# Cross-attention of a decoder block: turned maximum, softmax reciprocals and projection loads moved

## The chip, the cores and the metric

The kernel runs on one core of a Trainium2 chip. The metric is the device time of one execution in microseconds, the median over runs; lower is better.

## The reference

A decoder block with norms behind its residual sums: self-attention with fake quantisation to 8 bits, cross-attention, and a feed-forward net with low-rank additions. Eight batches of 512 tokens with 512 channels. The change is in the cross-attention, here cut to its core:

```python
q = (query @ Wq + bq).reshape(B, Nq, H, D).transpose(0, 2, 1, 3)      # B 8, Nq 512, H 16, D 32
k = (key_value @ Wk + bk).reshape(B, Nkv, H, D).transpose(0, 2, 1, 3)
v = (key_value @ Wv + bv).reshape(B, Nkv, H, D).transpose(0, 2, 1, 3)
attn = jnp.clip(jnp.einsum('bhqd,bhkd->bhqk', q, k) * scale, -CLAMP, CLAMP)
attn = jax.nn.softmax(attn, axis=-1)
x = jnp.einsum('bhqk,bhkd->bqhd', attn, v).reshape(B, Nq, Cq)
return x @ Wo + bo          # then: x2 = layernorm(x1 + this)
```

## The kernel before

The block is cut into stages with a barrier of all five engines between them; intermediate tensors go through device memory. Order within a stage is the order of each engine's own instruction list, tied by semaphores. SP issues nearly all the DMAs, in the order of its list, so a wait on SP holds every DMA behind it.

**Attention (between barriers 9 and 10).** 128 heads are 32 groups (GROUPS) of four. A group's queries and keys come as stacks of float16 halves (Qs, Ks; four slots), its values as vX (two slots). For each key tile c of four (NT), TensorE does in this order (group, line 981 on): score pair u = 0 of a head that is LEAD = 5 heads ahead, in banks 0 and 1, for the maximum alone (score_pair, L926); a quarter of the sums or values of the group before (values_of, L973); transposed key scores of this group (key_scores, L934) for two heads; score pair u = 1; key scores of the two other heads; minus the maximum added to all four by a matmul with ones (take_max, L942); another quarter of values_of. In the first two tiles values_of makes the softmax sums (bank 7), in the last two the values (bank 6). Behind the fourth tile the next group's maxima, which DVE has split in three bfloat16 parts (split_max, six small steps, L1593 to L1598, behind the third tile's reductions), are turned by four transposes (turn_max, L953) into bank 7, and ACT copies them to nmT (L1229).

DVE reduces each score pair to maxima (max_pair, L1583), which frees banks 0 and 1 for the next pair, and clips the exponentials of a tile in one step for all four heads (clip, L1604). ACT does the exponentials (L1235), the copies of values (values_out, L1223, at the start of a group) and sums (sums_out, L1216). SP's turn for a group (group_dma) waits for the last scores of that group, issues eight stack loads (L577) for the group four later, the next V load (L585), a store of the sums (L597) and a store of the undivided values (L591). After the last group all sums are loaded at once (L621), inverted by DVE (L1636) and stored (L625).

**Projection (between barriers 10 and 11).** SP loads Wo and bo (L632, L633), and per batch the values oK (L640), four broadcasts of reciprocals recK (L643) and the residual x1 into xK (L645). GpSimd multiplies oK by recK (L732), TensorE multiplies by Wo (L1024), DVE adds bo (L1646), adds the product (L1650) and norms; SP stores x2 (L649). Two slots each; a load of a batch waits for the store of x2 two batches before. ACT issues the loads of the two feed-forward weights, 4 MB each, behind the first xK loads (L1250).

Of the kernel before, what the change touches and what calls it, by code (L numbers as in the profile page):

```python
# [15 lines left out]
P = 128  # L16
# [14 lines left out]
XD = 32  # L31
# [42 lines left out]
def decoder(nc, x, ctx_768, g_ln, b_ln, w_qkv, w_out, log_temp, Wq, bq, Wk, bk, Wv, bv, Wo, bo,  # L74
# [22 lines left out]
    with ExitStack() as ctx:  # L97
# [234 lines left out]
        cX = Carve()  # L332
        Qs = cX(F16, 4, G, T)
# [5 lines left out]
        all_sums = cX(F32, T)  # L339
# [5 lines left out]
        nmT = cX(BF16, T)  # L345
# [3 lines left out]

        cK = Carve()  # L350
        Wo_s = cK(F32, KC, D)
        bo_s = cK(F32, D)
        oK = cK(F32, 2, KC, T)
        xK = cK(F32, 2, NT, D)
# [30 lines left out]
        recK = Carve(cW.at)(F32, 2, KC, T)  # L385
# [5 lines left out]
        def _(sp):  # L391
# [195 lines left out]
            def store_group(i, par):  # L587
                sp.wait_ge(S("oX_evac"), i + 1)
# [3 lines left out]

            def store_sums(i, par):
                sp.wait_ge(S("sumS_done"), i + 1)
                hold(sp)
                dst = sums_scr[i] if isinstance(i, int) else sums_scr[bass.ds(i, 1)].rearrange("a g t -> (a g) t")
                sp.dma_start(dst, sumS[0:P:XD, par, :]).then_inc(S(f"sums_stored{par}"), 16)  # L597
# [15 lines left out]
            with sp.Fori(1, GROUPS // 4 - 1) as j:  # L613
                for r in range(4):
                    group_dma(j * 4 + r, r)
            for i in range(GROUPS - 4, GROUPS):
                group_dma(i, i % 4)
            store_sums(GROUPS - 1, 1)
            for par in (0, 1):
                sp.wait_ge(S(f"sums_stored{par}"), 8 * GROUPS)  # L620
            sp.dma_start(all_sums, sums_scr.rearrange("a g t -> (a g) t")).then_inc(S("all_sums_in"), 16)  # L621
            for i in (GROUPS - 2, GROUPS - 1):
                store_group(i, i % 2)
            sp.wait_ge(S("rec_done"), 1)
            sp.dma_start(rec_scr.rearrange("a g t -> (a g) t"), all_sums).then_inc(S("rec_stored"), 16)  # L625
            for par in (0, 1):
                sp.wait_ge(S(f"oX_stored{par}"), 8 * GROUPS)
            sp.wait_ge(S("rec_stored"), 16)
            barrier(sp, 10)


            sp.dma_start(Wo_s, chunk(Wo)).then_inc(S("wI_in"), 16)  # L632
            sp.dma_start(bo_s, bo.rearrange("(a n) -> a n", a=1).broadcast_to([P, D])).then_inc(S("wI_in"), 16)  # L633

# [1186 lines left out]
```

## Time and profile before

| | us |
|---|---|
| median of 3 runs | 3690.12 (3690.01 to 3691.11) |
| profiled execution, time | 3690.49 |
| profiled execution, span | 3688.7 |
| TensorE matmul busy in the span | 2745.9 (74%) |
| DVE busy | 2574.5 (70%) |
| ACT busy | 1463.6 (40%) |
| GpSimd busy | 146.4 (4%) |
| attention, first to last matmul | 2153.2 to 2798.4 |
| projection, first to last matmul | 2834.2 to 3001.0 |

The profile is one execution; its rows are in microseconds from the start of the span. A timeline row gives start, length, engine, line, what is written from what, how many were merged, and in brackets how long the engine was idle before and what ended that. The mean granted clock of TensorE is a share of 2.4 GHz; 0.50 is 1.2 GHz. Busy shares are averages over stages with different limits, so each stage is read by itself.

### The profile page before, as it was taken

What the parts mean: (1) busy time and instruction counts of PE and PEld (TensorE: products, weight loads), DVE (VectorE), ACT (ScalarE), POOL (GpSimd) and SP (SyncE); (2) the same over time, 40 slices, a digit from 0 to 9 for tenths busy, and PEclk for the clock granted to TensorE, in tenths of its full rate; (3) what the DMA queues carried; (4) which work ended last, traced back from release to release, by engine and by line L of the source; (5) the groups of instructions that cost most, each with busy time, mean ns of one, the idle gap of its engine ahead of it and who ended that gap; (6) DMA issues with size and microseconds to landing.
All of it is one profiled execution on the core that took longest, in us unless ns stands there. A gap on an engine that the chain in (4) does not pass through costs nothing. (4 is left out here: it accounts for less than half of the span.)

```text
span 3688.7 us, 46276 instructions
## 1 busy us (share of the span) xinstructions
PE 2745.9 (74%) x13160; PEld 1067.8 (29%) x13160; DVE 2574.5 (70%) x4657; ACT 1463.6 (40%) x2397; POOL 146.4 (4%) x148
## 2 busy tenths in 40 slices
PE   1189999566664666664599969999995645999998
PEld 1134322111111433331244412222222223444443
DVE  6877799989887988884355547777773576455444
ACT  0000444489887988871122224444441001212221
POOL 0000333000000000000000000000001210000000
PEclk8599999555555989887799969999997877999999
DMA  5221221223232443434544433323325531001000
GB/s 199 74 91 46 92 116 78 103 102 112 100 105 90 135 126 125 129 111 183 193 165 166 175 86 84 84 75 82 86 63 194 182 121 35 24 23 36 33 23 23
DMA packets 199676, 375.20 MB, mean 102 GB/s; under 512 B 23680, under 2 KB 109696, under 8 KB 187136
## 3 DMA queue, kind: packets, MB, share of 16 engines
q1 hardware_dynamic: 195344, 357.03, 29.5%
q10 hardware_dynamic: 4208, 16.78, 1.2%
q8 instruction: 46, 0.75, 0.1%
q14 instruction: 78, 0.64, 0.1%
HBM read 218.02 MB, written 155.71 MB: 101 GB/s over the span
## 5 line engine op out<-in xcount | busy, mean ns | idle before, releaser
L1289 DVE TENSOR_REDUCE stats<-bank 128x1024 f32 (+1 forms) x352 | 407.9, 1216 | 65.5 <-PE bank L765 32.0
L1154 ACT ACTIVATE arena<-arena,scale 128x512 bf16<-128x512 int8 x512 | 410.1, 802 | 103.1 <-DVE arena L1476 94.4
L825 PE MATMUL bank<-arena 64*128 64x512 bf16 x512 | 306.2, 605 | 173.9 <-DVE arena L1471 138.8
L1583 DVE TENSOR_REDUCE arena<-bank 128x2 f32<-128x1024 f32 x256 | 312.8, 1222 | 136.3 <-PE bank L926 136.3
L1471 DVE CUSTOM_DVE_ANT_0 arena<-bank,arena,fac 128x512 int8<-128x512 f32 x512 | 353.9, 747 | 38.3 <-issue 17.8
L1169 ACT ACTIVATE arena<-arena,scale 128x512 f32<-128x512 int8 x512 | 366.4, 801 | 27.9 <-DVE arena L1497 14.8
L1235 ACT ACTIVATE arena<-bank 128x1024 f32<-128x1024 f32 x256 | 248.2, 1021 | 322.5 <-PE bank L942 322.5
L973 PE MATMUL bank<-arena 128*32 128x512 f32 x2048 | 272.0, 607 | 40.8 <-issue 32.7
L765 PE MATMUL bank<-arena 128*128 128x512 bf16 x1024 | 246.7, 386 | 59.9 <-DVE arena L1419 52.4
L845 PE MATMUL bank<-identb,arena 128*128 128x128 bf16 x2048 | 155.9, 237 | 172.1 <-DVE arena L1506 171.7
L1267 ACT ACTIVATE arena<-bank,arena,fac 128x512 f32<-128x512 f32 x128 | 99.5, 777 | 456.2 <-PE bank L1097 456.2
L1506 DVE TENSOR_SCALAR arena<-arena 128x512 bf16<-128x512 f32 x512 | 226.3, 481 | 43.5 <-ACT arena L1169 40.1
L1105 PE MATMUL bank<-arena 128*128 128x512 f16 x1024 | 242.0, 379 | 1.2 <-DVE arena L1767 0.8
L1094 PE MATMUL bank<-arena 128*128 128x512 f16 x1024 | 241.9, 379 | 0.0
L1766 DVE TENSOR_SCALAR arena<-arena 128x512 f16<-128x512 f32 x128 | 54.7, 427 | 260.0 <-ACT arena L1267 260.0
L845 PEld LDWEIGHTS bank<-identb,arena 128*128 128x128 bf16 x2048 | 132.2, 107 | 236.0 <-DVE arena L1506 146.3
L926 PE MATMUL bank<-arena 128*128 128x512 f16 x512 | 161.8, 399 | 42.3 <-DVE arena L1583 28.8
L1024 PE MATMUL bank<-arena 128*128 128x512 f32 x256 | 119.2, 628 | 83.4 <-POOL arena L732 83.4
L825 PEld LDWEIGHTS bank<-arena 64*128 64x128 bf16 x512 | 51.8, 101 | 428.3 <-DVE arena L1471 417.3
L1142 ACT ACTIVATE arena<-bank,floor_c,fac 128x1024 int8<-128x1024 f32 x96 | 115.6, 1205 | 150.1 <-PE bank L765 95.6
L1604 DVE TENSOR_SCALAR arena<-arena 128x2048 f32<-128x2048 f32 x128 | 155.8, 1217 | 13.3 <-ACT arena L1235 13.3
L934 PE MATMUL bank<-arena 128*128 128x512 f16 x512 | 157.2, 391 | 0.3
(189 smaller groups left out, 3585.1 us busy)
## 6 DMA issues: line engine op xcount, KB each, us to landing
dq_scr<-arena SPq DMA_DIRECT2D x128, 256.0 KB, 2.0
arena<-dq_scr SPq DMA_DIRECT2D x128, 256.0 KB, 2.7
arena<-half_scr SPq DMA_DIRECT2D x256, 128.0 KB, 2.8
qkv_scr<-arena SPq DMA_DIRECT2D x8, 3072.0 KB, 9.7
arena<-in_x SPq DMA_DIRECT2D x16, 1024.0 KB, 7.0
arena<-qkv_scr SPq DMA_DIRECT2D x128, 128.0 KB, 2.2
o_scr<-arena SPq DMA_DIRECT2D x64, 256.0 KB, 2.9
arena<-o_scr SPq DMA_DIRECT2D x8, 2048.0 KB, 9.2
```

The lines of the kernel that those rows point to most:

```text
L765: last = mm(dst, wqkv_q[:, k, P * u:P * u + P], hq[:, k, :], start=k == 0, stop=k == KC - 1)
L825: return mm(dst, qE[r, h // 2, P * t:P * t + P], kE[r, h // 2, :], start=True, stop=True)
L845: last = nc.tensor.transpose(PT[s % 2][:, j, P * t:P * t + P], aG[:, s % 2, t, P * j:P * j + P], identb[:, :])
L973: last = mm(bank[XD * g:XD * g + XD, 7 if k < 2 else 6, :], w, eT[:, par, g, c, :], start=c == 0, stop=c == NT - 1)
L1094: mm(dst, Wf[:, k, P * s:P * s + P], xx[:, par, k, :], start=k == 0 and n == 0, stop=False)
L1105: mm(bank[:, t, :], gg[:, f % 3, P * t:P * t + P], Wp[:, f, :], start=f == 0 and n == 0, stop=False)
L1154: last = A(e_dump[:, NT * (h % 2) + t, :], dq8[:, h % 4, t, :], ACT.Exp, bias=negm_b[:, par, c:c + 1], scale=scale[:, S_DOTS:S_DOTS + 1], ...
L1169: A(eG[:, s % 2, t, :], dqG[:, s % 4, t, :], ACT.Exp, bias=negm_g[:, par, c:c + 1], scale=scale[:, S_DOTS:S_DOTS + 1]).then_inc(S("eG_done ...
L1235: A(eT[:, r % 2, 2 * a:2 * a + 2, c, :], bank[:, 2 + 2 * a:4 + 2 * a, :], ACT.Exp, scale=XSCALE / HALF ** 2).then_inc(S("eX_done"), 1)
L1289: return V.tensor_reduce(dst, src, ax, ALU.max, apply_absolute_value=True)
L1471: V.tensor_tensor_reduce(dq8[:, s, t, :], bank[:, 4 * (h % 2) + t, :], floor_row, fac[:, C_DOTS:C_DOTS + 1], -3.0e38, ALU.add, ALU.max, ac ...
L1583: V.tensor_reduce(mxX[:, mp, hs, 2 * u:2 * u + 2], bank[:, 0:2, :], AX.X, ALU.max).then_inc(S("sX_red"), 1)
```

## The change

In the attention: the turn of the next maximum moves on TensorE from behind the last key tile to inside it, ahead of its key scores, and its copy on ACT ahead of that tile's exponentials, with nmT in two slots. The split on DVE is cut in two parts of three steps, with a reduction between. Clips of the first and last tile are done in halves. The sums of a group go through memory one group at a time: store, load spread over 128 partitions with 16 columns each, reciprocal on DVE in the group two later, store, broadcast back to recB, and GpSimd multiplies the evacuated values before they are stored. The last two groups are inverted and multiplied by DVE. In the projection nothing is divided any more; its tiles lie at the top of the arena, and its weights and first two batches are loaded before the last four groups. Values of batch b+2 are loaded once batch b's matmuls are done, x1 once its x2 is stored.

```diff
             def store_group(i, par):
-                sp.wait_ge(S("oX_evac"), i + 1)
+                sp.wait_ge(S("oX_ready"), i + 1)
                 hold(sp)
...
+            def load_spread(i, par):
+                sp.wait_ge(S(f"sums_stored{par}"), i * 8 + 16 - 8 * par)
+                hold(sp)
+                sp.dma_start(sums16, spread(sums_scr, i)).then_inc(S("sums16_in"), 16)
+
+            def store_rec(i):
+                sp.wait_ge(S("rec_done"), i + 1)
+                hold(sp)
+                sp.dma_start(spread(rec_scr, i), sums16).then_inc(S("rec_stored"), 16)
+
+            def load_rec(i, par):
+                sp.wait_ge(S("rec_stored"), i * 16 + 16)
+                hold(sp)
+                for g in range(G):
+                    row = rec_scr[i, g:g + 1, :] if isinstance(i, int) else rec_scr[bass.ds(i, 1), g, :]
+                    sp.dma_start(recB[XD * g:XD * g + XD, par, :], row.broadcast_to([XD, T])).then_inc(S(f"rec_in{par}"), 16)
...
             def group_dma(i, r):
-                if not (isinstance(i, int) and i + 4 >= GROUPS):
+                known = isinstance(i, int)
+                if not (known and i + 4 >= GROUPS):
                     load_stacks(i + 4, r)
-                if not (isinstance(i, int) and i + 1 >= GROUPS):
+                if not (known and i + 1 >= GROUPS):
                     load_v(i + 1, (r + 1) % 2)
-                if not (isinstance(i, int) and i < 1):
+                if not (known and i < 2):
+                    store_rec(i - 2)
+                if not (known and i < 3):
+                    store_group(i - 3, (r + 1) % 2)
+                if not (known and i < 1) and not (known and i == GROUPS - 1):
                     store_sums(i - 1, (r + 1) % 2)
-                if not (isinstance(i, int) and i < 2):
-                    store_group(i - 2, r % 2)
+                if not (known and i < 2):
+                    load_rec(i - 2, r % 2)
+                if not (known and i < 1) and not (known and i == GROUPS - 1):
+                    load_spread(i - 1, (r + 1) % 2)
...
+            sp.dma_start(Wo_s, chunk(Wo)).then_inc(S("wI_in"), 16)
+            sp.dma_start(bo_s, bo.rearrange("(a n) -> a n", a=1).broadcast_to([P, D])).then_inc(S("wI_in"), 16)
+            for b in (0, 1):
+                load_values(b, b)
+                load_x1(b, b)
             for i in range(GROUPS - 4, GROUPS):
                 group_dma(i, i % 4)
...
+            def after_batch(b, par):
+                sp.wait_ge(S("wo_mm"), b * NT + NT)
+                hold(sp)
+                load_values(b + 2, par)
+                store_x2(b, par)
+                sp.wait_ge(S(f"x2_stored{par}"), b * 8 + 32 - 8 * par)
+                load_x1(b + 2, par)
...
+            def divide(i, par):
+                pool.wait_ge(S(f"rec_in{par}"), (i * 8 + 16 - 8 * par) * G)
+                pool.wait_ge(S("oX_evac"), i + 1)
+                hold(pool)
+                nc.gpsimd.tensor_tensor(oX[:, par, :], oX[:, par, :], recB[:, par, :], ALU.mult).then_inc(S("oX_ready"), 1)
...
                     if previous:
                         values_of(i - 1, (r + 1) % 2, c, 0)
+                    if c == NT - 1 and not (isinstance(i, int) and i == GROUPS - 1):
+                        turn_max(i + 1)
                     key_scores(i, r, c, 0)
...
                     if previous:
                         values_of(i - 1, (r + 1) % 2, c, 1)
-                if not (isinstance(i, int) and i == GROUPS - 1):
-                    turn_max(i + 1)
...
             def group(i, r):
-                if not (isinstance(i, int) and i < 2):
-                    values_out(i - 2, r)
-                act.wait_ge(S("nmT_mm"), i + 1)
-                A(nmT, turned_max, ACT.Copy).then_inc(S("nmT_ready"), 1)
                 for c in range(NT):
+                    if c == 0 and not (isinstance(i, int) and i < 2):
+                        values_out(i - 2, r)
...
+                    if c == NT - 1 and not (isinstance(i, int) and i == GROUPS - 1):
+                        max_turned(i + 1, 1 - r)
...
+            def invert(i):
+                dve.wait_ge(S("sums16_in"), i * 16 + 16)
+                V.reciprocal(sums16, sums16).then_inc(S("rec_done"), 1)
...
-                        if u == 0:
-                            clip_before(i, r, c)
-                    if c == 2 and not (isinstance(i, int) and i == GROUPS - 1):
-                        split_max(i + 1, (r + 1) % 2)
+                        if c == 0 and not first:
+                            clip(i - 1, 1 - r, NT - 1, u)
+                        if c == 1:
+                            clip(i, r, 0, u)
+                        if (c, u) == (2, 0):
+                            clip(i, r, 1, None)
+                        if (c, u) == (2, 1) and not last:
+                            split_max(i + 1, 1 - r, True, False)
+                        if (c, u) == (3, 0) and not last:
+                            split_max(i + 1, 1 - r, False, True)
+                        if (c, u) == (3, 1):
+                            clip(i, r, 2, None)
+                        if (c, u) == (0, 1) and not (isinstance(i, int) and i < 2):
+                            invert(i - 2)
...
-            clip(GROUPS - 1, 1, NT - 1)
-            dve.wait_ge(S("all_sums_in"), 16)
-            V.reciprocal(all_sums, all_sums).then_inc(S("rec_done"), 1)
+            for a in (0, 1):
+                clip(GROUPS - 1, 1, NT - 1, a)
+            for i in (GROUPS - 2, GROUPS - 1):
+                dve.wait_ge(S("sumS_done"), i + 1)
+                link(V.reciprocal(sumS[:, i % 2, :], sumS[:, i % 2, :]))
+                dve.wait_ge(S("oX_evac"), i + 1)
+                dve.wait_ge(S("oX_ready"), i)
+                V.tensor_tensor(oX[:, i % 2, :], oX[:, i % 2, :], sumS[:, i % 2, :], ALU.mult).then_inc(S("oX_ready"), 1)
```

## Rows read from the trace of the kernel before

**Rows 1.** Windows: one group; length, busy by engine (instructions), granted clock, DMA share, GB/s.
```profile
2507.24:2526.50 19.26, 17.50 (x120) 4.22 (x116) 15.12 (x18) 9.23 (x12) 0.00 (x0) 1.00 0.29 82
```

**Rows 2.** Timeline around the start of a group, TensorE, ACT and SP.
```profile
2505.92 0.40 PE L942 MATMUL bank<-arena 3*128 3x512 bf16 x4
2506.62 3.66 SPq L577 DMA_DIRECT2D arena<-half_scr  x8
2507.25 0.40 PE L953 MATMUL bank<-identb,arena 128*128 128x128 bf16 x4
2509.37 1.06 PE L973 MATMUL bank<-arena 128*32 128x512 f32 x8 [1.30 <-issue]
2511.16 0.57 SPq L597 DMA_DIRECT2D sums_scr<-arena  x1
```

**Rows 3.** Timeline of a middle key tile, score pairs and reduction.
```profile
2513.09 0.61 PE L926 MATMUL bank<-arena 128*128 128x512 f16 x2
2515.07 0.59 PE L926 MATMUL bank<-arena 128*128 128x512 f16 x2
2517.35 0.60 PE L926 MATMUL bank<-arena 128*128 128x512 f16 x2
2517.99 1.23 DVE L1583 TENSOR_REDUCE arena<-bank 128x2 f32<-128x1024 f32 x1 [0.77 <-PE bank L926]
```

**Rows 4.** Timeline of a last key tile.
```profile
2502.39 0.60 PE L926 MATMUL bank<-arena 128*128 128x512 f16 x2
2502.44 0.17 DVE L1593 TENSOR_SCALAR arena<-arena 128x16 f32<-128x16 f32 x1 [0.18 <-DVE arena L1583]
```

**Rows 5.** Waits of SP over 2200 to 2780: total us, times, longest.
```profile
SPq L231 <- PE bank L942: 359.1, 27, 16.8
```

**Rows 6.** DMAs: stacks' landing times; two issues at the seam (KB, landing); one broadcast set.
```profile
DMA to landing us min/median/max: 2.1/2.8/4.3
...
arena<-sums_scr SPq DMA_DIRECT2D x1, 256.0 KB, 2.9
rec_scr<-arena SPq DMA_DIRECT2D x1, 256.0 KB, 2.0
...
2807.46 2.60 SPq L643 DMA_DIRECT2D arena<-rec_scr  x4
```

**Rows 7.** Windows of one us behind group 30, columns as in rows 1.
```profile
2776.00:2777.00 1.00, 0.00 (x0) 0.00 (x0) 0.89 (x1) 1.00 (x3) 0.00 (x0) 1.00 0.72 158
2777.00:2778.00 1.00, 0.84 (x5) 0.23 (x8) 0.34 (x1) 0.06 (x1) 0.00 (x0) 0.53 0.82 311
...
2780.00:2781.00 1.00, 1.00 (x7) 0.11 (x5) 0.00 (x0) 0.00 (x0) 0.00 (x0) 0.77 0.00 0
```

**Rows 8.** Timeline of the seam between attention and projection.
```profile
2790.47 7.95 PE L973 MATMUL bank<-arena 128*32 128x512 f32 x72
2792.54 1.23 DVE L1604 TENSOR_SCALAR arena<-arena 128x2048 f32<-128x2048 f32 x1 [1.93 <-ACT arena L1235]
2800.43 3.35 DVE L1636 RECIPROCAL arena<-arena 128x512 f32<-128x512 f32 x1 [6.66 <-DMA arena<-sums_scr]
2834.23 6.23 PE L1024 MATMUL bank<-arena 128*128 128x512 f32 x9 [35.82 <-POOL arena L732]
```

**Rows 9.** Projection: its window, columns as in rows 1, and timeline rows.
```profile
2834.20:3001.10 166.90, 119.25 (x256) 51.24 (x256) 91.73 (x228) 0.00 (x0) 36.59 (x28) 0.84 0.63 206
...
2903.31 0.37 SPq L649 DMA_DIRECT2D x_scr<-arena  x1
2921.50 4.96 DVE L1646 TENSOR_TENSOR arena<-arena 128x512 f32<-128x512 f32 x4 [4.40 <-DMA arena<-x_scr]
2950.02 2.49 DVE L1646 TENSOR_TENSOR arena<-arena 128x512 f32<-128x512 f32 x4
2979.41 20.76 PE L1024 MATMUL bank<-arena 128*128 128x512 f32 x48
```

More of the change, by code:

```diff
@@ L338, in decoder @@
         sumS = cX(F32, 2, T)
-        all_sums = cX(F32, T)
+        recB = cX(F32, 2, T)
+        sums16 = cX(F32, G * T // P)
         mxX = cX(F32, 2, G, NT)
@@ L649, in store_x2 @@
                 sp.dma_start(at4(x2_scr, b), xK[:, par]).then_inc(S(f"x2_stored{par}"), 16)
-            ahead(sp, load_values, store_x2)
+            def after_batch(b, par):
[5 more added lines that the diff above has]
+                load_x1(b + 2, par)
+            with sp.Fori(0, NB // 2 - 1) as j:
+                after_batch(j * 2, 0)
+                after_batch(j * 2 + 1, 1)
+            store_x2(NB - 2, 0)
+            store_x2(NB - 1, 1)
             for par in (0, 1):
@@ L941, in take_max @@
                     q = slice(XD * g, XD * g + 3)
-                    last = mm(bank[:, 2 + g, :], ones_b[q, :], nmT[q, :], start=False, stop=True)
+                    last = mm(bank[:, 2 + g, :], ones_b[q, :], nmT[q, r % 2, :], start=False, stop=True)
                     if g % 2:
@@ L1601, in clip @@
[L1601 to L1611 removed]
+                if first:
+                    dve.wait_ge(S("sX_red"), i * 8 + 8)
+                    if not (isinstance(i, int) and i == 0):
+                        dve.wait_ge(S("nmT_mm"), i)
+                    hold(dve)
+                    ch.link(V.tensor_scalar(capX, mxX[:, mp], XSCALE / HALF ** 2, CLIP_SPAN - CLAMP, ALU.mult, ALU.max))
+                    ch.link(V.tensor_scalar(negX, capX, CLAMP, -(HALF ** 2) / XSCALE, ALU.min, ALU.mult))
+                    ch.link(V.tensor_copy(slots[:, :, :, 0], by_tile(negX)))
@@ new lines, in split_max, with clip @@
+                ch.n = 3
+                if second:
+                    ch.link(V.tensor_tensor(by_tile(restX), by_tile(negX), slots[:, :, :, 0], ALU.subtract))
+                    ch.link(V.tensor_copy(slots[:, :, :, 1], by_tile(restX)))
+                    V.tensor_tensor(slots[:, :, :, 2], by_tile(restX), slots[:, :, :, 1], ALU.subtract).then_inc(S("nm_ready"), 1)
+                    ch.end()
+            def clip(i, r, c, a):
+                heads = slice(0, G) if a is None else slice(2 * a, 2 * a + 2)
+                n = 2 if a is None else 1
+                dve.wait_ge(S("eX_done"), i * 8 + 2 * c + (a or 0) + n)
+                e = eT[:, r, heads, c, :]
+                V.tensor_scalar(e, e, CLIP_FLOOR, 1.0, ALU.max, ALU.min).then_inc(S("clipped"), n)
@@ L1613, in group @@
+            def invert(i):
+                dve.wait_ge(S("sums16_in"), i * 16 + 16)
+                V.reciprocal(sums16, sums16).then_inc(S("rec_done"), 1)
             def group(i, r):
+                first, last = (isinstance(i, int) and i == k for k in (0, GROUPS - 1))
                 for c in range(NT):
```

108 lines of the change are left out of this document (38 added, 70 removed).

## The prediction

> **What bounds the kernel now.** I read the page's slices first, then the windows by stage, the timeline of one attention group, the waits of the DMA queue, and the timeline of the seam behind the attention. In the cross-attention a group of four heads takes 19.26 us with TensorE busy 17.50, DVE 15.12, ACT 9.23 [rows 1]. Within a group a middle key tile takes 4.26 us, from 2513.09 to 2517.35, and the next maximum reduction starts 0.64 us behind its score pair, which it had waited for [rows 3]: TensorE is the bound there. Four tiles and the turn (0.23 us) would be 17.27; the group has two holes besides. At its start TensorE waits for the evacuation of the turned maximum: turn at 2507.25, next value matmul 2509.37; the first tile takes 5.6 us in place of 4.26 [rows 2]. In the last tile six small DVE steps stand ahead of the reduction that frees the score banks, and it takes 4.86 us (2502.39 to 2507.25) [rows 2, 4]. Together 2.0 us. Behind the attention TensorE stands still from 2798.42 to 2834.23, 35.8 us, and the projection then takes until 3001.1 with TensorE busy 119 of 167 us at a mean clock of 0.84 [rows 8, 9].
>
> **The turn and the splits.** The turn moves into the last tile, ahead of its key scores, so its evacuation is hidden: minus 1.35 us. But it needs the second half of the split, which now stands behind the reduction of that tile's first score pair. Counted from the third tile's first matmul: the last tile's begins at 4.26, its reduction runs about 4.98 to 6.20, three small steps of 0.17 to 0.23 us with gaps take 0.70; the first of them is in [rows 4], so the turn can begin at 7.0. TensorE is there at 5.80: pair, value matmuls and two key scores take 1.98 (2513.09 to 2515.07), the key scores alone some 0.44 of it [rows 3]. It waits 1.2 us, where it lost 0.6. Net minus 0.8 a group: 18.5 us if nothing else waits. The clip in halves and the split in parts only fill DVE's idle 0.6 to 0.8 us behind each reduction; with TensorE as the bound they give nothing more.
>
> **The way of the sums through memory.** This is the term that decides. SP runs its list in order. Its turn for a group begins when the group's last scores are done (first stack issue at 2506.62, 0.70 behind the start of the last maximum matmuls), and before the change it then has slack: over 27 groups it waited 359 us for that event, 13.3 each [rows 2, 5]. Call this start s; the next group's first score pair, F, is at s + 0.63 once the turn is gone from there (0.33 for the maxima and 1.0 for the values behind 2505.92). In the changed list the load of group i-2's sums for the reciprocal stands last in the turn of group i-1, and DVE waits for it in group i behind its second reduction. So it is not a whole group of slack but the first few us of a group. The chain:
> - eight stack issues and the V load: 4.54 us until the next issue (2506.62 to 2511.16) [rows 2], now the store of the previous reciprocals;
> - SP waits for that store to land. No row shows it beside the stacks: alone a store to this tensor took 2.0, a stack under the same burst 2.8 in the median, 4.3 at most [rows 6]. I take 2.8, as this one is queued behind the burst. The stores of values and sums are issued in that time;
> - four row broadcasts: 2.60 for four such issues; eight stack issues took 3.66, so 1.83 is the low end [rows 2, 6]; 3.2 the high end, by estimate from these;
> - the load itself: 2.9 for the load of all sums [rows 6], 2.0 to 4.3 as bounds; small gaps between issues 0.3.
>
> Sum 4.54 + 2.8 + 2.6 + 2.9 + 0.3 = 13.1 us behind s (10.7 to 16.6). DVE gets there on its own at F + 4.5 = s + 5.1: two reductions, each 0.64 behind its pair, the second pair at F + 1.98, and half a clip of 0.61. So DVE waits some 8 us (5.6 to 11.5) every group. Queued behind it is the next reduction, and behind that, on TensorE, the second score pair of the second tile. The reciprocal of 16 columns is 3.35 / 32 [rows 8] plus a fixed part, 0.3 us; then 1.22 for the reduction and 0.12. The pair starts at s + 14.8 = F + 14.2; from there 2.28 us finish the tile (2515.07 to 2517.35) and 4.26 + 5.70 the other two. Group: 26.4 us, 7.1 more than now.
>
> ACT has a wait of the same kind: evacuating the values of group i-2 needs group i-4's store, which has moved one turn later and behind the stacks: about s + 5.4 + 2.8, evacuation and first exponentials at s + 9.9. TensorE needs these for the key scores of the second tile, which it reaches before the late score pair at s + 14.8: hidden. The GpSimd division takes 1.3 us (36.59 / 28) [rows 9], in a time when its core has nothing else, and nobody waits for it but SP one turn later.
>
> **The clock.** For 7.6 us TensorE would have two matmuls. In this trace an idle stretch of 1.7 us behind group 30 was enough: granted 1.00 in the idle us, 0.53 in the next, 0.77 in the fourth [rows 7], so 3.7 us at 1.2 GHz. That loses 1.9 us of TensorE's work, and TensorE is the bound behind the wait. Group: 28.3 us.
>
> The sum: groups 3 to 28 have the full chain, 26 x (28.3 - 19.26) = 235. Group 2 has no reciprocals to store ahead, 2.7 us shorter: +6. Groups 29 and 30 have no stacks ahead, 3.9 us shorter: +10. Group 31 +1, groups 0 and 1 together -1.6. Attention +251.
>
> **Seam and projection.** Operands, bias and the first two batches are loaded in the attention. After its last matmul comes on DVE the tail of two reciprocals of 3.35 and two products of 0.7; the first starts behind the last clip (2792.54 and 1.23), 4.6 us before the end, so the last product ends 3.8 behind it, and with a store of 2.9 and the barrier it is 7.3 us [rows 6, 8]. The projection itself: 48 matmuls in 20.76 us [rows 9] are 0.43 each, 32 a batch, 13.8 us; eight batches 110.1, plus 1.9 for a slow clock at the start and 3 for x1 tiles that arrive late beside the two 4 MB weight loads, which now start at once (an estimate, 0 to 8). DVE is busy 91.7 us in eight batches, 11.5 each, under 13.8. From a store of x2 to the adds on the x1 that waits for it is 18.2 us now (2903.31 to 2921.50), with 2 MB of values and reciprocals ahead in the queue; without them it should fit in the other batch's 13.8. From the last attention matmul to the last projection matmul: 7.3 + 115 = 122.3, now 202.7. Gain 80. The removed GpSimd scaling stood between load and matmul and is in this figure. Cover for the early loads: 5.25 MB at about 0.3 MB a us is 17 us, in front of group 28's turn, inside a group's length; without that cover they cost some 4 us once.
>
> Profiled execution: span 3688.7, time 3690.5, against a median of 3690.1. 3690.5 + 251 - 80 = 3861 us. The unknown transfers alone move it from 3791 to 3955.
>
> The Trainium skill, DMA: Bandwidth & Descriptors, section "Anatomy of one DMA", gives a DMA a fixed cost of about 2.0 us that does not grow with size, most of it the receipt of the write. By that both waits would be 2.0, the group about 1.7 us shorter, and the time about 3815; the lone store agrees at 2.0, the stacks in the burst do not (2.8).
>
> **Rivals.**
> - A: the wait is there but the clock holds. For it: granted clock 1.00 all through a group that has a hole of 1.3 us [rows 1, 2]. Against it: rows 7, with a shorter idle time than I expect. Group 26.4 us, attention +195, time 3805; with the shortest transfers 3737.
> - B, on the other side: the transfers are covered, DVE finds its sums in place, and the change does what it says. Then 18.5 us a group, attention -25, time 3585. It decides at a chain of s + 8.8 us: there the group is 22.1 us and pays back the 80. For it: 13 us of slack on SP. Against: this slack lies ahead of s, not behind it, and the stacks alone take 3.7.
> - C: GpSimd's division holds DVE up as well. Beside such products DVE's four bias adds took 4.96 us, alone 2.49 [rows 9]. Up to 1.3 us a group, 26 x 1.3 = 34: 3895. Against: it falls where DVE waits or reads PSUM. The Trainium skill, SBUF — State Buffer, section "Who interferes with whom", has the two engines share a port pair that one instruction holds whole; the trace agrees, with 4.96 against 2.49.
>
> **Chances.** Forecast 0.60 (3790 to 3955), A 0.22 (3737 to 3830), C 0.08, B 0.10. The range of 8 in 10 takes the forecast's and A's cases but for their far ends: 3750 to 3930. About 0.2% is what a measurement of this kernel tells from no change. Slower by over that 0.90 (forecast, A, C), within it 0.01, faster 0.09 (B, with a little left for something between).
>
> **What would show it.** A DVE wait of some 8 us for a load of the sums in each of groups 2 to 28, and TensorE idle behind it; group length near 28 us; granted clock down to about 0.5 for 3 to 4 us in each group. The turn waiting about 1.2 us for DVE in the last tile. ACT's evacuation of the values waiting for a store of two groups before, with nobody behind. At the seam under 10 us, and the projection at 13.8 us a batch without TensorE's holes of 15 us. Wrong it would be if SP reaches the load of the sums within 6 us, if two landings together take under 2 us, or if DVE's wait lies where TensorE has work that needs neither score banks nor exponentials.

## The result and the profile of the changed kernel

The changed kernel takes 3807.3 us in the median (3804.1 to 3810.4), the kernel before 3690.6 beside it: a ratio of 1.031, interval 1.030 to 1.032. It is slower by 117 us, inside the range of the prediction and 54 us under its 3861. The profiled execution took 3804.1 us with a span of 3802.1, which is 113.4 more than before. All of it lies in two places: the attention, first to last matmul, takes 844.4 us instead of 645.2 (plus 199.2), and from its last matmul to the last of the projection it is 116.9 instead of 202.7 (minus 85.8).

Windows of the changed kernel: 25 groups of the attention (turn to turn), one group of them, three stretches within it, and the projection. Columns as in rows 1.
```profile
2260.52:2932.24 671.72, 506.79 (x2900) 111.57 (x2901) 388.50 (x525) 235.21 (x275) 31.52 (x25) 0.85 0.28 76
2611.22:2636.82 25.60, 19.56 (x116) 4.41 (x117) 15.50 (x21) 9.33 (x11) 1.26 (x1) 0.87 0.27 73
2622.00:2623.00 1.00, 0.18 (x1) 0.13 (x2) 0.00 (x0) 1.00 (x2) 0.00 (x0) 0.77 0.37 127
2623.00:2629.00 6.00, 3.94 (x14) 0.74 (x16) 3.76 (x5) 1.29 (x2) 1.26 (x1) 0.50 0.07 17
2629.00:2630.00 1.00, 1.00 (x9) 0.11 (x2) 0.00 (x0) 1.00 (x2) 0.00 (x0) 0.82 0.00 0
3001.90:3113.50 111.60, 111.53 (x256) 49.21 (x256) 86.54 (x231) 0.00 (x0) 0.00 (x0) 0.99 0.68 254
```
A group takes 671.72 / 25 = 26.9 us where it took 19.26 [rows 1]. TensorE is busy 506.79 / 25 = 20.3 us of it, before 17.5, at a mean clock of 0.85, before 1.00. So of the 7.6 us more, 2.8 are the same matmuls run slower and 4.8 are idle time (6.6 now, 1.8 before). The projection is now full: 111.53 busy of 111.60, where it was 119 of 167 [rows 9].

Waits of the changed kernel over the same 25 groups: who waits for whom, us in total, times, longest.
```profile
DVE arena L1650 <- DMA arena<-sums_scr: 159.7, 25, 7.6
ACT arena L1254 <- DMA oT_scr<-arena: 159.3, 25, 8.1
PE bank L968 <- ACT arena L1270: 78.2, 25, 4.8
PE bank L960 <- DVE arena L1620: 59.7, 25, 2.9
PE bank L987 <- DVE arena L1638: 27.2, 25, 1.2
SPq L231 <- PE bank L976: 408.7, 25, 16.8
```
Every group has the new wait of DVE's reciprocal (L1650) for the load of its sums, 6.4 us in the mean. It has a second one that looks just as large: ACT's evacuation of the values (L1254) for a store of two groups before. SP itself still stands idle 408.7 us for the last scores of a group, 16.3 each, as in [rows 5]: its slack is there, but behind the list and not ahead of it.

Timeline of one group of the changed kernel, the rows in the order of the chain. L987 is the turn, L960 a score pair, L968 the key scores, L1620 the maximum reduction, L1650 the reciprocal; on SP L578 is the stacks, L586 V, L613 the store of reciprocals, L592 and L603 those of values and sums, L620 the broadcasts, L608 the load of sums.
```profile
2611.22 0.38 PE L987 MATMUL bank<-identb,arena 128*128 128x128 bf16 x4 [1.01 <-DVE arena L1638]
2613.52 3.65 SPq L578 DMA_DIRECT2D arena<-half_scr  x8
2614.15 0.61 PE L960 MATMUL bank<-arena 128*128 128x512 f16 x2
2617.44 0.35 SPq L586 DMA_DIRECT2D arena<-v_scr  x1
2618.17 0.38 SPq L613 DMA_DIRECT2D rec_scr<-arena  x1
2618.91 0.35 SPq L592 DMA_DIRECT2D oT_scr<-arena  x1
2620.72 1.91 SPq L620 DMA_DIRECT2D arena<-rec_scr  x4
2621.25 0.60 ACT L1254 ACTIVATE arena<-bank 128x512 f32<-128x512 f32 x1 [6.05 <-DMA oT_scr<-arena]
2622.82 1.04 PE L968 MATMUL bank<-arena 128*128 128x512 f16 x2 [2.80 <-ACT arena L1270]
2622.88 0.36 SPq L608 DMA_DIRECT2D arena<-sums_scr  x1
2624.50 1.26 POOL L764 TENSOR_TENSOR arena<-arena 128x512 f32<-128x512 f32 x1 [25.39 <-DMA arena<-rec_scr]
2624.52 0.25 DVE L1650 RECIPROCAL arena<-arena 128x16 f32<-128x16 f32 x1 [5.93 <-DMA arena<-sums_scr]
2624.69 1.17 DVE L1620 TENSOR_REDUCE arena<-bank 128x2 f32<-128x1024 f32 x1
2625.92 1.04 PE L960 MATMUL bank<-arena 128*128 128x512 f16 x2 [2.06 <-DVE arena L1620]
2628.28 1.57 PE L1004 MATMUL bank<-arena 128*32 128x512 f32 x8
2636.82 0.38 PE L987 MATMUL bank<-identb,arena 128*128 128x128 bf16 x4 [1.18 <-DVE arena L1638]
```
SP's turn starts at s = 2613.52, the next scores at F = 2614.15, 0.63 later. The reciprocal's sums are there at 2624.52 = s + 11.0. Behind it come the reduction and, at 2625.92, the late score pair, F + 11.8. TensorE had two holes ahead of it, 2.80 and 2.06 us, with one key score pair between them. The eight value matmuls at L1004 behind take 1.57 us at the lower clock and 1.06 to 1.07 elsewhere in the group. The turn waits 1.0 to 1.2 us for DVE's last split step (L1638).

Timeline of the seam in the changed kernel.
```profile
2988.69 7.93 PE L1004 MATMUL bank<-arena 128*32 128x512 f32 x72
2998.75 0.69 DVE L1691 TENSOR_TENSOR arena<-arena 128x512 f32<-128x512 f32 x1
3001.96 111.53 PE L1055 MATMUL bank<-arena 128*128 128x512 f32 x256 [5.33 <-POOLq L235]
```
The hole of 35.8 us [rows 8] is 5.3, and the 256 matmuls of the projection run in one piece.

### The profile page after: what moved, and what is told of

Its sections match the earlier page's. It is cut to its first block and busy times, and to the rows that moved or that the text cites. A ratio compares the mean times of both kernels' runs of the same rounds, so it can differ in the third digit from the quotient of the medians.

```text
span 3802.1 us, 46990 instructions
## 1 busy us (share of the span) xinstructions
PE 2799.9 (74%) x13113; PEld 1070.7 (28%) x13160; DVE 2583.6 (68%) x4754; ACT 1468.5 (39%) x2397; POOL 143.2 (4%) x146
## 3 DMA queue, kind: packets, MB, share of 16 engines
q1 hardware_dynamic: 204832, 356.46, 28.3%
## 5 line engine op out<-in xcount | busy, mean ns | idle before, releaser
L1620 DVE TENSOR_REDUCE arena<-bank 128x2 f32<-128x1024 f32 x256 | 311.7, 1218 | 151.3 <-PE bank L960 144.1
L1004 PE MATMUL bank<-arena 128*32 128x512 f32 x2048 | 297.7, 661 | 0.0
L960 PE MATMUL bank<-arena 128*128 128x512 f16 x512 | 181.5, 442 | 100.4 <-DVE arena L1620 86.7
L1125 PE MATMUL bank<-arena 128*128 128x512 f16 x1024 | 243.1, 381 | 0.0
L1136 PE MATMUL bank<-arena 128*128 128x512 f16 x1024 | 242.0, 379 | 1.2 <-DVE arena L1822 0.7
L968 PE MATMUL bank<-arena 128*128 128x512 f16 x512 | 174.1, 427 | 80.1 <-ACT arena L1270 79.8
L1646 DVE TENSOR_SCALAR arena<-arena 128x1024 f32<-128x1024 f32 (+1 forms) x192 | 166.7, 869 | 4.5 <-ACT arena L1270 4.5
L1549 DVE TENSOR_SCALAR arena<-bank 128x2048 bf16<-128x2048 bf16 x128 | 155.8, 1217 | 1.9 <-PE bank L879 0.7
```

Source lines behind the costliest of these rows:

```text
L1004: last = mm(bank[XD * g:XD * g + XD, 7 if k < 2 else 6, :], w, eT[:, par, g, c, :], start=c == 0, stop=c == NT - 1)
L1125: mm(dst, Wf[:, k, P * s:P * s + P], xx[:, par, k, :], start=k == 0 and n == 0, stop=False)
L1136: mm(bank[:, t, :], gg[:, f % 3, P * t:P * t + P], Wp[:, f, :], start=f == 0 and n == 0, stop=False)
L1620: V.tensor_reduce(mxX[:, mp, hs, 2 * u:2 * u + 2], bank[:, 0:2, :], AX.X, ALU.max).then_inc(S("sX_red"), 1)
```

## The experiments

My theory: the whole loss is the two waits through memory that SP's list puts into the first microseconds of a group, DVE's first of all, with the clock behind it. The rivals: the wait is there but something else holds the group (ACT's wait, GpSimd's division, the split of the DVE work); or the clock has no part in it. The kernel before was measured beside every experiment, with medians of 3691.1 to 3692.5.

**The reciprocal later on DVE.** The kernel change with one condition moved: the reciprocal comes in the last key tile in place of the first.
```diff
-                        if (c, u) == (0, 1) and not (isinstance(i, int) and i < 2):
+                        if (c, u) == (3, 0) and not (isinstance(i, int) and i < 2):
                             invert(i - 2)
```


> Edit: the reciprocal of group i-2's sums moves on DVE from behind the second reduction of group i to behind the seventh (last tile); SP's list stays. DVE's wait for the sums (6.4 us a group in the changed kernel's trace) should be gone, ACT's wait for the store of the values of group i-4 stays. Theory (two waits side by side, the longer hides the shorter): key scores of the second tile are then late by 2.9 us; group 21.4 us while the clock holds, 3664 us; 23.2 us with a dip of the clock, 3711 us. Rival (DVE's wait alone makes the loss, ACT's is free): 18.5 us a group, 3584 us. Rival (DVE's place in the list doesn't matter, the memory traffic does): 3807 us, unchanged.

Measured: 3688.6 us, ratio to before 0.9994 (0.9985 to 1.0004), groups of 21.4 to 24.0 us from group 4 to group 28. DVE's wait is gone, and 119 us with it, but ACT's is not. Timeline of this kernel, the same place in a group:
```profile
2513.45 0.60 ACT L1254 ACTIVATE arena<-bank 128x512 f32<-128x512 f32 x1 [5.96 <-DMA oT_scr<-arena]
2515.01 0.60 PE L968 MATMUL bank<-arena 128*128 128x512 f16 x2 [2.72 <-ACT arena L1270]
2518.98 0.95 PE L960 MATMUL bank<-arena 128*128 128x512 f16 x2
```
TensorE now waits 2.7 us for the exponentials behind the late evacuation, and the 0.95 of the last row, 0.60 elsewhere, is the lower clock again (mean over 2400 to 2700: 0.95). The time lies between the two that were expected with the clock up and down.

**The store of values first in SP's turn**, the reciprocal left where the change has it.
```diff
             def group_dma(i, r):
                 known = isinstance(i, int)
+                if not (known and i < 3):
+                    store_group(i - 3, (r + 1) % 2)
...
                 if not (known and i < 2):
                     store_rec(i - 2)
-                if not (known and i < 3):
-                    store_group(i - 3, (r + 1) % 2)
```


> Edit: the store of group i-3's values moves to the head of SP's turn, ahead of the wait for the last scores and of the stack loads; the reciprocal stays early. ACT's wait should be gone, DVE's stays. Theory (DVE's wait is the longer and hides ACT's): the late score pair still starts 11.8 us into the group, group 26.9 us, 3807 us, within 15 us. Rival (ACT's wait is on the path as well, the two add up): 2.9 us less a group, about 3730 us.

Measured: 3801.8 us, ratio 1.030 (1.028 to 1.031), groups of 25.7 to 27.6. ACT's wait for that store is gone, and the time is only 5.5 us below the changed kernel's, with ratios whose intervals overlap. Waits of this kernel over 2260 to 2740:
```profile
DVE arena L1650 <- DMA arena<-sums_scr: 114.1, 18, 7.7
```
In the changed kernel ACT's wait lies inside DVE's. It costs next to nothing while DVE's is there.

**Both edits together.**

> Edit: both moves of the two runs before in one kernel. Neither wait is left. Theory (these two waits and the clock that falls in them are the whole loss): 18.5 us a group at a granted clock of 1.00, 3580 us (3570 to 3600), faster than both kernels. Rival (the memory traffic, the division on GpSimd or the halved clips slow the group as well): 19.3 us a group or more, 3605 us or more.

Measured: 3587.6 us, ratio 0.972 (0.970 to 0.973). The two edits bring 119 and 5.5 us alone and 219.7 together: the early store, worth 5.5 us while DVE waits, is worth 101 (3688.6 to 3587.6) once DVE doesn't. Most groups take 18.48 us at a clock of 1.00, as the prediction had it for a group where nothing else waits (18.5), and the time is 2.6 us from its rival B (3585). This is what the change gives once its two transfers come in time. Group 29 is out of line: it took 26.49 us, with ACT waiting 9.04 us once for the store of values. That store stood in the queue right behind the early loads. Four more groups of the profiled execution (14, 15, 16 and 26) took 19.5 to 19.6 us. Timeline of this kernel in group 14:
```profile
2450.83 1.26 POOL L764 TENSOR_TENSOR arena<-arena 128x512 f32<-128x512 f32 x1 [16.10 <-DMA arena<-rec_scr]
2450.87 2.30 DVE L1646 TENSOR_SCALAR arena<-arena 128x2048 f32<-128x2048 f32 x1
2454.36 0.61 PE L960 MATMUL bank<-arena 128*128 128x512 f16 x2 [0.95 <-DVE arena L1620]
```
In these four the division on GpSimd started 0.03 to 0.09 us ahead of DVE's wide clip, the clip took 2.26 to 2.32 us in place of 1.22, and in the row above TensorE then waits 0.95 us for the reduction behind it. In the groups of 18.5 us from 5 to 28 the clip started first and kept its 1.22. That is rival C of the prediction, at 1.1 us for a group that it hits.

**The chain first.** The reciprocal stays early on DVE. In SP's turn the stores, the four broadcasts and the load of sums now come ahead of V and the stacks.
```diff
             def group_dma(i, r):
                 known = isinstance(i, int)
+                if not (known and i < 3):
+                    store_group(i - 3, (r + 1) % 2)
                 if not (known and i + 4 >= GROUPS):
-                    load_stacks(i + 4, r)
-                if not (known and i + 1 >= GROUPS):
-                    load_v(i + 1, (r + 1) % 2)
+                    sp.wait_ge(S("sT_mm"), i * 8 + 8)
+                    hold(sp)
                 if not (known and i < 2):
                     store_rec(i - 2)
-                if not (known and i < 3):
-                    store_group(i - 3, (r + 1) % 2)
...
                     load_spread(i - 1, (r + 1) % 2)
+                if not (known and i + 1 >= GROUPS):
+                    load_v(i + 1, (r + 1) % 2)
+                if not (known and i + 4 >= GROUPS):
+                    load_stacks(i + 4, r)
```


> Edit: the changed kernel with the reciprocal at its early place on DVE, but in SP's turn the way of the sums (store of reciprocals, store of sums, broadcasts, spread load) stands ahead of the V load and the eight stack loads, behind the same wait for the last scores; the store of the values is at the head. The chain of memory steps from the start of SP's turn should shrink from 11.0 to some 6.4 us. Theory (the group's loss is the chain's end minus DVE's arrival at 5.1): DVE waits 1.3 us, 19.7 us a group, clock 1.00, 3618 us, faster than before though the wait is still there. Rival (any wait of DVE at this place costs several us, by the clock or by the traffic): 22 us or more a group, 3690 us or more.

Measured: 3594.7 us, ratio 0.974 (0.972 to 0.975), groups of 18.5 to 19.6 (group 29 again apart, 30.1). Timeline of this kernel (its L1653 is the reciprocal):
```profile
2514.36 0.37 SPq L613 DMA_DIRECT2D rec_scr<-arena  x1
2515.97 1.91 SPq L620 DMA_DIRECT2D arena<-rec_scr  x4
2518.13 0.36 SPq L608 DMA_DIRECT2D arena<-sums_scr  x1
2519.86 0.25 DVE L1653 RECIPROCAL arena<-arena 128x16 f32<-128x16 f32 x1 [0.41 <-DMA arena<-sums_scr]
```
The chain takes 5.5 us from its first issue, and DVE, which the prediction had there 5.1 us behind s, waits 0.41. The kernel with only the store of values first (two experiments above) differs from this one in that order alone and took 3801.8 us, 207 more. The wait of the changed kernel is thus a matter of order in one queue: the same transfers, issued ahead of the nine others, cost almost nothing. Of the 5.5 us by which the chain is shorter than the changed kernel's 11.0, 4.65 are the nine issues and 0.94 the store of reciprocals, behind which the broadcasts now go out 1.61 us later and not 2.55. The expectation (19.7 a group) had the chain at 6.4.

**The waits kept, their holes filled.** The changed kernel, with 15 more 128x512 matmuls a group into a free bank: 4 behind the wait for ACT's late evacuation, 11 behind the next key scores, where TensorE waits for DVE.
```diff
+                    late = c == 1 and not (isinstance(i, int) and i < 3)
+                    if late:
+                        pe.wait_ge(S("oX_evac"), i - 1)
+                        fill(r, 4)
                     key_scores(i, r, c, 0)
+                    if late:
+                        fill(r, 11)
```


> Edit: the changed kernel, both waits in place, with 15 matmuls of 128x512 float16 more in the second tile of groups 3 to 31, four ahead of the key scores and eleven behind them, into the bank of the values, whose next accumulation starts afresh; so TensorE works through most of its wait. The output is the same. Theory (of 26.9 us a group 2.8 are the clock's fall in the wait): clock near 1.00, 24.1 us a group, 26 x 2.8 = 73 us faster than the changed kernel in spite of 435 matmuls more, 3730 us. Rival (the clock's fall costs nothing, the group waits for DVE and memory): 26.9 us a group, 3807 us or more.

Measured: 3764.4 us, ratio 1.019 (1.018 to 1.021). Windows of this kernel, 2400 to 2700 and one group:
```profile
2400.00:2700.00 300.00, 255.29 (x1574) 69.69 (x1573) 186.06 (x252) 111.94 (x133) 15.17 (x12) 0.98 0.27 75
2539.40:2564.50 25.10, 21.32 (x137) 5.91 (x135) 15.50 (x21) 9.69 (x12) 1.26 (x1) 1.00 0.28 74
```
Timeline of the same kernel, the fillers (L1011) and the late pair:
```profile
2550.07 1.02 PE L1011 MATMUL bank<-arena 128*128 128x512 f16 x4 [2.11 <-ACT arena L1265]
2551.36 2.54 PE L1011 MATMUL bank<-arena 128*128 128x512 f16 x11
2554.38 0.61 PE L960 MATMUL bank<-arena 128*128 128x512 f16 x2 [0.49 <-DVE arena L1631]
```
435 more matmuls, and the kernel is 43 us faster than the changed one; the waits stay (DVE 6.6 us each, 131.9 in 20). The clock is 0.98 in place of 0.85, and a group 25.2 us in the mean in place of 26.9. So the clock's share is real, 1.7 us a group at least: more than that cannot be read here, as the clock still falls in some groups (a mean of 0.93 or 0.94 in 11 of the 26 from 3 to 28, 1.00 in the others). I had expected 3730. The wait itself is as long as it was, F to the late pair 12.3 in this group, and sets 24.5 or more with the 12.2 us of work behind.

**The turn and the split as before.** Both edits of above, but the turn, its copy and the six unsplit small steps at their old places.
```diff
-                    if c == NT - 1 and not (isinstance(i, int) and i == GROUPS - 1):
-                        turn_max(i + 1)
+                if not (isinstance(i, int) and i == GROUPS - 1):
+                    turn_max(i + 1)
...
-                            split_max(i + 1, 1 - r, True, False)
+                            split_max(i + 1, 1 - r, True, True)
```


> Edit: the kernel with both waits removed (e3_both), with the turn of the maximum, its copy and the unsplit six steps put back to their places of the kernel before. Theory (the turn's part is worth 0.8 us a group): 19.3 us a group, 3587 + 25 = 3612 us. Rival (with both waits gone the place of the turn is hidden, or the split maximum is what costs): 18.5 us a group, 3587 us or less.

Measured: 3618.1 us, ratio 0.980 (0.978 to 0.981), groups of 19.24 us in the mode, where the kernel before has 19.26 [rows 1]. Against 18.48 with the moved turn the move is worth 0.76 a group, predicted 0.8, and 30.6 us in all, where 25 were expected; 4.9 of them lie in groups 0 and 1 and 1.6 in group 29.

**The turn behind the second score pair.** Both edits, and the turn some 0.9 us of TensorE's work later, so that DVE's last split step is ready.
```diff
-                    if c == NT - 1 and not (isinstance(i, int) and i == GROUPS - 1):
-                        turn_max(i + 1)
                     key_scores(i, r, c, 0)
                     if scores:
                         score_pair(ahead_h, ahead_r, hs, 1)
+                    if c == NT - 1 and not (isinstance(i, int) and i == GROUPS - 1):
+                        turn_max(i + 1)
```


> Edit: as the run before, and the turn of the next maximum stands behind the second score pair of the last tile in place of before the key scores. Theory (the turn waits 1.2 us for DVE's second half of the split, which 0.87 us of other matmuls can cover): 17.6 us a group, 3553 us. Rival (DVE's steps, not the turn's place, set the last tile): 18.5 us a group, 3580 us.

Measured: 3560.5 us, ratio 0.964 (0.963 to 0.966), groups of 17.62: the turn's wait for DVE, predicted and measured at 1.2 us, was on the path, and 0.86 of it is to be had. Window of this kernel:
```profile
2400.00:2660.00 260.00, 257.83 (x1708) 59.83 (x1708) 229.77 (x310) 138.02 (x163) 31.55 (x15) 1.00 0.38 104
```
Timeline of the same kernel, the early loads (L654 is the first of them), the store behind them and ACT's evacuation:
```profile
2685.15 0.41 SPq L654 DMA_DIRECT2D arena<-in_L_xattn_Wo  x1
2689.03 0.44 SPq L592 DMA_DIRECT2D oT_scr<-arena  x1
2704.32 0.60 ACT L1254 ACTIVATE arena<-bank 128x512 f32<-128x512 f32 x1 [9.80 <-DMA oT_scr<-arena]
```
TensorE is busy 257.83 of 260 us. Group 29 still took 26.45, with ACT 9.80 us late; its 8.8 us more than another group account for the 7.5 above the 3553 expected. Groups 6, 9 and 21 took 18.6 to 18.7 us, each with the division started 0.02 to 0.13 us ahead of the wide clip and a clip of 2.2 to 2.3 us.

**The early loads late.** Both edits, with Wo, the bias and the first two batches loaded behind the attention's last barrier.
```diff
-            sp.dma_start(Wo_s, chunk(Wo)).then_inc(S("wI_in"), 16)
-            ... bo; for b in (0, 1): load_values(b, b); load_x1(b, b)
             for i in range(GROUPS - 4, GROUPS): ...
             (barrier)
+            sp.dma_start(Wo_s, chunk(Wo)).then_inc(S("wI_in"), 16)
+            ... bo; for b in (0, 1): load_values(b, b); load_x1(b, b)
```


> Edit: e3_both with Wo, bo and the first two batches of values and x1 loaded behind the barrier that ends the attention. Theory (the early loads hide some 13 us at the seam, and cost 8 us once in group 29, whose value store waits behind 5.25 MB in the queue): the first projection matmul comes 13 to 15 us later, group 29 is 8 us shorter; 3587 + 6 = 3593 us (3588 to 3600). Rival (the early loads are the larger part of the seam's gain of 30 us): 3587 + 20 us or more.

Measured: 3592.6 us, ratio 0.973 (0.972 to 0.975), 5 us above the same kernel with the early loads. First projection matmul of this kernel:
```profile
2788.71 21.54 PE L1055 MATMUL bank<-arena 128*128 128x512 f32 x45 [14.84 <-DMA arena<-oT_scr]
```
The early loads save 9.5 us at the seam (14.84 less 5.33), where 13 to 15 were expected, and group 29 is 18.49 without them, so they cost 8.0 there; the two places account for 1.5 of the 5 us, and the intervals of the two kernels overlap. Of the 30.5 us that the hole at the seam shrank by, only 9.5 are the loads; the other 21.0 (35.82 to 14.84) come with the division done ahead, with no set of reciprocals to store, broadcast and multiply by.

**The early loads in three parts.** The kernel with the turn behind the second score pair; Wo and the bias ahead of group 28, one batch behind its turn, one behind the next.
```diff
-            for b in (0, 1):
-                load_values(b, b)
-                load_x1(b, b)
             for i in range(GROUPS - 4, GROUPS):
                 group_dma(i, i % 4)
+                if i < GROUPS - 2:
+                    load_values(i % 4, i % 4)
+                    load_x1(i % 4, i % 4)
```


> e4_turn_later with the first batch of the projection's early loads issued one group later and the second batch two groups later (Wo and bo stay where they are). In e4_turn_later the group after the early loads took 26.45 us against 17.62 for the others, because the value store landed 9.8 us late behind 5.25 MB of loads. Theory (the loads in one lump are the cause): each group sees a third of the bytes, the value store lands in time or nearly so, that group takes 18 to 19 us, and the time is 3552 us (3550 to 3555). Rival (the same bytes only move the wait into the two groups behind, or to the seam, where the first projection matmul then waits for x1): 3560 us, with the 8 us found in those groups or ahead of the first projection matmul.

Measured: 3551.8 us, ratio 0.963 (0.961 to 0.964): the fastest that ran with its output whole. Group 29 takes 17.62 like all others, and the hole at the seam stays at 5.33. The lump was the cause.

**What the division costs.** The same kernel with the GpSimd product cut to 32 of 512 columns, so that the output of 30 groups is left undivided in all other columns.
```diff
-                nc.gpsimd.tensor_tensor(oX[:, par, :], oX[:, par, :], recB[:, par, :], ALU.mult)
+                nc.gpsimd.tensor_tensor(oX[:, par, 0:32], oX[:, par, 0:32], recB[:, par, 0:32], ALU.mult)
```


> e9_loads_spread with the GpSimd division in the attention cut to the first 32 of its 512 columns, so the output of 30 of the 32 groups is divided in part only; waits, signals and stores stay. It measures what the division itself costs. Theory (it lies beside DVE work that has slack, TensorE is the bound): groups of 17.6 us as before, 3552 us, within 3 of e9_loads_spread. Rival C of the prediction (it takes a port from DVE and holds the reductions up, up to 1.3 us a group): groups of 16.3 to 17.3 us and a time of 3510 to 3545 us.

Measured: 3550.2 us (3547.3 to 3551.4), ratio 0.962 (0.961 to 0.963), the same within the measurement; groups of 17.62. Instructions grouped by line and shape over 2400 to 2654 (count, busy us, mean ns, idle before), of the kernel with the full product:
```profile
L1646 DVE TENSOR_SCALAR arena<-arena 128x2048 f32<-128x2048 f32 x29 | 35.3, 1216 | 0.0
L764 POOL TENSOR_TENSOR arena<-arena 128x512 f32<-128x512 f32 x15 | 32.0, 2136 | 232.2 <-DMA arena<-rec_scr 232.2
```
Of the kernel with the small product:
```profile
L1646 DVE TENSOR_SCALAR arena<-arena 128x2048 f32<-128x2048 f32 x29 | 35.3, 1216 | 0.0
L764 POOL TENSOR_TENSOR arena<-arena 128x32 f32<-128x32 f32 x14 | 14.1, 1008 | 232.5 <-DMA arena<-rec_scr 232.5
```
DVE's wide clips, the work that the product runs beside, have the same length in both. That doesn't exclude rival C: in the profiled execution of the full product the division never started ahead of a wide clip in groups 5 to 28, so there was nothing to win there. With the small product it did so in groups 8 and 20, by 0.14 and 0.12 us, and they took 17.62 all the same, its 0.25 us being short. Where the full product is first, a group is 1.0 to 1.1 us longer, as the traces of the two kernels above show.

## Why the prediction held, and where its terms were off

**The sign and the mechanism: right.** The prediction named the one chain that decides, DVE's wait for the sums of two groups before, ahead of the maximum reductions, and priced it above the 80 us of the seam. The reciprocal moved alone gives 119 us back, both transfers in time 220. The slack of SP is on the other side of s, as it had argued from [rows 5].

**The chain: 11.0 us in place of 13.1.** The point at which it starts (s + 4.65, predicted 4.54) was right, but every transfer was quicker: the store of reciprocals until the broadcasts go out 2.55 (2618.17 to 2620.72; taken 2.8), the broadcasts 1.91 (2.6), the load 1.64 (2622.88 to 2624.52; 2.9). The last two are the step that failed. For the broadcasts I took the four at the seam [rows 6], though the eight stack issues of the same burst gave 1.83, and for the load the landing of a transfer of 256 KB, 2.9 us; the load of 16 columns took 1.64. The Trainium skill, DMA: Bandwidth & Descriptors, section "Anatomy of one DMA", has about 2.0 us as a DMA's fixed cost. The section gives it for DMAs that GpSimd issues, and these are SP's. The two landings are 4.2 together and it would have had 4.0, against my 5.7, though neither is 2.0 itself.

**The clock: 2.8 us a group in place of 1.9.** That it falls was right: 0.77 in the us in which the first hole ends, 0.50 in the next six, 0.82 in the eighth. I had taken the length of the dip, some 3.7 us, from behind a hole of 1.7 [rows 7]. I misread these rows: with the two us between them at 0.50 each they give 0.94 + 1 + 1 + 0.46 = 3.4 us at the low clock (a us with a mean of 0.53 is 0.94 us at 0.50 and the rest at 1.00) and 1.7 us of work lost, not 3.7 and 1.9. Here two holes of 2.8 and 2.1 us follow each other, and 6 us pass at half speed. Busy time per group is 2.8 above that of [rows 1]; the filled kernel gives back 1.7 of it in time, and the rest I can't place.

**The sum of a group.** Predicted 28.3 us: 19.4 busy and 8.9 idle. Measured 26.9: 20.3 busy and 6.6 idle. Over 26 groups that is 37 us of the 52 by which the attention was overestimated. Groups 29 and 30, 20.4 and 20.0 in place of 24.4, are 8 more: they have no stacks ahead of the chain, DVE waits 2.3 and 3.2 us, and the clock holds. Group 2 took 21.5 in place of 25.6, 4 more. Window of group 29 of the changed kernel:
```profile
2932.30:2952.60 20.30, 17.44 (x116) 1.00 0.23 82
```
Its columns are length, TensorE busy, clock, DMA share, GB/s.

**ACT's wait: right in this kernel, incomplete as an account.** Evacuation at s + 7.7 and key scores at s + 9.3 (predicted 9.9), hidden to 5.5 us of 117. But "nobody behind" was wrong: TensorE waits for it 3.1 us in every group (78.2 in 25), and would have waited for DVE in the same stretch anyway. Once DVE's is gone it is worth 101 us. A reader who repairs DVE's wait only gets the kernel before, not a faster one.

**The turn: right.** It waits 1.0 to 1.2 us; 18.5 us a group if nothing else waits is 18.48.

**Seam and projection: minus 85.8, predicted minus 80.** The hole is 5.3 us (7.3 predicted): last product at 2.8 us behind the last matmul and not 3.8, and the barrier opens 2.5 behind it, for which I had 3.5 with a store of 2.9; the 2.9 in [rows 6] is a load, the store there took 2.0. The projection takes 111.5 (115): no x1 tile is late, the 3 us for them were too many, and no slow clock shows at its start (0.99).

**The early loads: hidden here, for a reason that I hadn't given.** They cost nothing in the changed kernel because its groups were waiting anyway. With the waits gone, group 29 is 8 us longer, where I had 4 us without cover. They don't take up the length of a group; they hold back the one store that stands behind them in the queue.

**Rivals.** A (3805) comes nearest to the time, by two errors that cancel: the clock does not hold, the transfers are shorter than in its sum. B is what the kernel with both transfers in time shows, 3587.6 against its 3585, and that this is so close is luck too: the attention gained 15 us and not 25, for group 29 and the groups that C hit, and seam and projection 84 and not 80. In the changed kernel the chain was over 2.2 us behind s + 8.8, where by my sum the group's loss would have eaten the gain of the seam. C did not occur in the changed kernel, whose division lies 5 to 8 us ahead of the wide clip from group 4 to group 30 (1.26 and 1.22 us). It is real where the waits are gone: 1.0 to 1.1 us in a group where the division starts first, in four of the groups 5 to 28 with both edits, in three with the turn behind the second pair and in none of the fastest kernel's profiled execution. It is not in every group, as the rival had it.

Open is how the clock's fall depends on the pattern of holes: in the filled kernel some groups keep 1.00 and others have 0.93, with the same instructions. Open is also what decides in a given group whether the division or the clip starts first.

## What to carry to other kernels

A transfer that is "two groups ahead" in the data can still be late by its place in an in-order queue: before moving one, write down the event that the queue waits for and add up what is issued between that event and the transfer. When a trace shows two waits of the same length in the same stretch, one may be worth next to nothing alone (5.5 us here) and a great deal once the other is gone (101 us); try both at once. Large prefetches ahead of a small store that an engine of the running loop waits for are better issued in parts. When a few groups of a loop are longer than the rest, look at them one by one: here they show a contention that the mean hides.

## What the runs showed of the hardware

- A hole of 2.8 us in TensorE's work was followed by a granted clock of 0.77 in the us of its end and of 0.50 for the next 6 us, although matmuls ran again for 3.9 of them. Work in the holes (15 matmuls in 4 us) kept it at 0.98.
- GpSimd's 128x512 product took 1.26 us beside DVE's reciprocal of 16 columns and a reduction out of PSUM, and 2.1 in the mean where it meets DVE's wide clip. Timeline of the fastest kernel, one group:
```profile
2507.93 1.22 DVE L1646 TENSOR_SCALAR arena<-arena 128x2048 f32<-128x2048 f32 x1
2508.21 2.07 POOL L764 TENSOR_TENSOR arena<-arena 128x512 f32<-128x512 f32 x1 [15.55 <-DMA arena<-rec_scr]
```
The clip was first and kept its 1.22 us; the product ends 1.13 us behind the end of the clip (2510.28 against 2509.15), as if it had begun only there. With the product first, by 0.04 us, it was the reverse (the kernel with both edits, group 14): product 1.26, clip 2.30. In the kernel before, GpSimd was running first and both paid, DVE the more: 4.96 against 2.49 for its adds [rows 9], GpSimd 5.81 for four products where 4.94 is usual. Timeline of the kernel before:
```profile
2919.51 5.81 POOL L732 TENSOR_TENSOR arena<-arena 128x512 f32<-128x512 f32 x4 [24.63 <-DMA arena<-rec_scr]
```
The Trainium skill, SBUF — State Buffer, section "Who interferes with whom", says that the one that issued first holds the shared port pair for its whole instruction and the other blocks; these rows agree with it, and it makes rival C a question of who starts first.
- The store of values, which ACT doesn't wait for in any other group from 2560 on in the trace of the kernel with the turn behind the second score pair, kept it waiting 9.8 us behind 5.25 MB of loads issued in the 4 us ahead of it.
